# Two Mamba mixers on one core: the second token tile's state part moved ahead of the first tile's sums of squares

## What is computed

```
proj = x @ in_proj            # z (1024), xBC (1024 + 2N), dt (heads)
xBC  = silu(conv4(xBC) + b)   # causal, 4 taps, per channel
dt   = softplus(dt + bias);   state_t = exp(dt*A) * state + dt*x_t B_t
y_t  = C_t . state_t + D*x_t
A:  out = rmsnorm(y * silu(z)) @ out_proj      (16 heads of 64, N = 64)
B:  out = (rmsnorm(y) * silu(z)) @ out_proj    (64 heads of 16, N = 128)
```

## Time and profile before

| | us |
|---|---|
| three executions | 2859.62, 2861.10, 2862.26 (median 2861.1) |
| profiled execution, span | 2859.7 |
| TensorE matmul busy | 2733.3 (96%) |
| TensorE weight load busy | 1845.0 (65%) |
| VectorE busy | 2009.9 (70%) |
| ScalarE busy | 1527.0 (53%) |
| GpSimd busy | 926.1 (32%) |
| mean granted TensorE clock | 0.980 of 2.4 GHz |

### The profile page before, as it was taken

How to read it: one execution, slowest core, us unless ns; L and a number is a source line. 1 busy time by engine, 2 the same in 40 slices (tenths; PEclk the granted TensorE clock), 3 DMA queues, 4 the chain that set the end, 5 groups by cost and what they waited for, 6 DMA issues and landing times. The chain is left out here.

```text
span 2859.7 us, 49906 instructions
## 1 busy us (share of the span) xinstructions
PE 2733.3 (96%) x17464; PEld 1845.0 (65%) x17464; DVE 2009.9 (70%) x3695; ACT 1527.0 (53%) x2418; POOL 926.1 (32%) x614
## 2 busy tenths in 40 slices
PE   7999999999999999996899999999999999997996
PEld 6777766777766665455666666666666666664453
DVE  5666666666666663377788888888888888885267
ACT  3444444445455442341577666766667776665242
POOL 2222223222223321232233444333333334332134
PEclk9999999999999999998999999999999999998998
DMA  4000000000000034145000000000000000022333
GB/s 125 23 23 22 22 22 22 23 28 29 22 22 22 16 121 152 45 147 204 12 23 22 22 22 16 21 22 22 15 15 22 22 22 22 15 95 89 112 118 133
DMA packets 79935, 139.59 MB, mean 49 GB/s; under 512 B 17896, under 2 KB 17896, under 8 KB 78832
## 3 DMA queue, kind: packets, MB, share of 16 engines
q1 hardware_dynamic: 70752, 125.92, 12.9%
q10 hardware_dynamic: 9104, 12.63, 1.4%
HBM read 104.98 MB, written 33.55 MB: 48 GB/s over the span
## 5 line engine op out<-in xcount | busy, mean ns | idle before, releaser
L655 PE MATMUL work<-b_xnT,shared_w 128*128 128x256 f32 x2304 | 545.8, 388 | 1.8 <-DVE b_parts L1192 1.3
L655 PE MATMUL work<-a_xnT,shared_w 128*128 128x256 f32 x2176 | 509.4, 392 | 1.3
L655 PEld LDWEIGHTS work<-b_xnT,shared_w 128*128 128x128 f32 x2304 | 426.1, 191 | 90.6 <-issue 30.1
L655 PEld LDWEIGHTS work<-a_xnT,shared_w 128*128 128x128 f32 x2176 | 419.0, 195 | 73.8 <-issue 12.3
L1232 DVE TENSOR_TENSOR b_decay<-b_decay,b_gt 128x1024 f32<-128x1024 f32 x256 | 351.7, 1395 | 119.3 <-ACT b_decay L943 115.8
L936 ACT ACTIVATE b_decay<-seg 128x1024 f32<-128x1024 f32 x256 | 248.5, 1029 | 112.0 <-PE seg L781 111.8
L943 ACT ACTIVATE b_decay<-b_decay 128x1024 f32<-128x1024 f32 x256 | 266.1, 1073 | 0.0
L1406 POOL TENSOR_TENSOR b_rhs<-b_l_side,of_head 128x1024 fp32r<-128x1024 f32 x32 | 82.0, 2563 | 552.4 <-DVE b_l_side L1201 552.4
L1441 POOL TENSOR_TENSOR a_y<-a_y,a_skip 128x1024 f32<-128x1024 f32 x32 | 90.9, 2840 | 484.1 <-DVE a_y L1221 484.1
L1111 DVE SCALAR_TENSOR_TENSOR shared_cv<-shared_pre,a_conv_w,shared_cv 128x256 f32<-128x256 f32 x432 | 189.7, 482 | 74.6 <-ACT shared_cv L880 68.9
L1111 DVE SCALAR_TENSOR_TENSOR shared_cv<-shared_pre,b_conv_w,shared_cv 128x256 f32<-128x256 f32 x480 | 232.1, 517 | 14.2 <-ACT shared_cv L880 6.3
(11 more groups left out here) (314 smaller groups left out, 4612.4 us busy)
## 6 DMA issues: line engine op xcount, KB each, us to landing
shared_x<-in_L_attn_a_x SPq DMA_DIRECT2D x16, 512.0 KB, 3.5
a_x_res<-in_L_attn_a_x SPq DMA_DIRECT2D x32, 256.0 KB, 2.6
x_mid<-a_x_res SPq DMA_DIRECT2D x32, 256.0 KB, 2.1
shared_w<-in_L_ffn_d_w SPq DMA_DIRECT2D x2, 4096.0 KB, 14.0
f_d_w<-in_L_ffn_d_w SPq DMA_DIRECT2D x2, 4096.0 KB, 14.5
f_x_res<-x_mid SPq DMA_DIRECT2D x8, 1024.0 KB, 5.9
f_bc_w<-x_mid SPq DMA_DIRECT2D x8, 1024.0 KB, 5.6
shared_x<-x_mid SPq DMA_DIRECT2D x16, 512.0 KB, 3.6
```

The costliest lines, as they stand in the source:

```text
L655: mm = nc.tensor.matmul(dst, w_in[:, k, col:col + m], xnT[:, k, :], start=(k == 0), stop=(k == KD - 1))
```

## The change

On TensorE the steps `z0a, z0b, rs0, yoff1a, yoff1b, seg1.0, rt0, out0` become `z0a, yoff1a, yoff1b, rs0, seg1.0, z0b, rt0, out0`. The banks follow from the order. The use two before: for yoff1a it is state0 (state0b in mixer B) instead of z0b, for yoff1b z0a instead of rs0, for rs0 yoff1a instead of z0a, for z0b yoff1b instead of the state step, for rt0 rs0 instead of yoff1a, for out0 z0b instead of yoff1b. ScalarE copies z0b after the two bounds instead of ahead of them. VectorE runs `from_state(1)` ahead of `square_sums`, and in mixer B (NP = 4) the conv of the last two blocks comes after `square_sums` instead of ahead of `from_state`. In the last super-tile, without z and conv work, the order changes from `rs0, yoff1a, yoff1b, seg1.0, rt0` to `yoff1a, yoff1b, rs0, seg1.0, rt0`. No instruction is added or removed.

```diff
@@ -463,8 +463,8 @@
                 if p + 1 == NP:
                     steps += state_steps(0)
                 steps += [f"ydiag0.{2 * p}", f"ydiag0.{2 * p + 1}"]
-            steps += ["z0a", "z0b"] if nxt else []
-            steps += ["rs0", "yoff1a", "yoff1b", "seg1.0", "rt0", "out0"]
+            steps += (["z0a"] if nxt else []) + ["yoff1a", "yoff1b", "rs0", "seg1.0"]
+            steps += (["z0b"] if nxt else []) + ["rt0", "out0"]
             for p in range(NP):
@@ -1005,10 +1005,10 @@
                     square(2 * i)
                     if nxt:
                         z_copy(sec, "z0a")
+                    slot_bound(sec, 1, 0)
+                    slot_bound(sec, 1, 1)
                     if nxt:
                         z_copy(sec, "z0b")
-                    slot_bound(sec, 1, 0)
-                    slot_bound(sec, 1, 1)
                     slot_exp(sec, 1, 0)
                     slot_exp(sec, 1, 1)
                     out_rsqrt(2 * i)
@@ -1313,8 +1313,10 @@
                             if g + 1 == NS and NP > 1:
                                 state_add(sec, 0)
                                 gate(sec, 0)
-                            for k in range(0, len(blks), 2):
-                                conv_blocks(sec, blks[k:k + 2])
+                            late = blks if g + 1 == NS and NP > 1 else []
+                            if not late:
+                                for k in range(0, len(blks), 2):
+                                    conv_blocks(sec, blks[k:k + 2])
@@ -1323,8 +1325,10 @@
                     if NP == 1:
                         state_add(sec, 0)
                         gate(sec, 0)
+                    from_state(sec, 1)
                     square_sums(sec, "rs0")
-                    from_state(sec, 1)
+                    for k in range(0, len(late), 2):
+                        conv_blocks(sec, late[k:k + 2])
                     rms_var(sec, "rt0")
                     slot_mult(sec, 1, 0)
                     slot_mult(sec, 1, 1)
```

## The result

The changed kernel takes 2869.1 us (median of six executions, 2866.7 to 2877.9) against 2861.2 us (six of the kernel before, 2859.5 to 2862.3): a ratio of 1.0031, 95% interval 1.002 to 1.0043. It is slower by 7.9 us. The profiled execution is one of the fastest (2866.7 us, span 2864.9), so its 5.2 us over the span of before are less than the median shows.

A forecast was written before the change was run, and what follows sets the result against it. TensorE, its matmuls busy 96% of the span, was taken as the bound. 19.4 - 1.0 - 6.1 = +12.3 on the profiled 2859.7 gave 2872.0, with 1.4 for the runs' median 2873 us; range 2865 to 2884.

The forecast's parts named there:

- The mechanism in A: Mixer A's 15 super-tiles: yoff1b waits for z0a's copy, out0 for z0b's; loss 1.29 us each, +19.4 us.
- The unseen step: TensorE's step from rs0 to seg1.0, not in the trace: taken as 0.58 us, bounds 0.38 and 1.14.
- Mixer B: Its 15 super-tiles: yoff1b doesn't wait, out0 at 7.17 us after z0a instead of 7.27; -0.07 each, -1.0 us.
- The conv's cover: VectorE in mixer B: the later conv, 3.84 us, even at 1.5 times, ends before out0 has ended; cost 0.
- The last super-tiles: Without z work, state parts fill TensorE's wait for the squares: gain 2.5 us in A, 3.6 in B, 6.1 together.
- The clock in A's loop: Low-clock stretches in 7 of mixer A's 15 super-tiles, 1.69 us each: number left at 7, ±8.4 us.
- rival 2: No change: mixer A's low-clock stretches fall to nearly none, -8 to -12 us, time 2861 to 2866; 12%.
- Rival 3: TensorE's new idle stretch in many of A's super-tiles brings the low clock: up to 25 us more, 2885 to 2898; 12%.
- Rival 1: Mixer A's loss is absorbed by TensorE's headroom, under 0.5 us a super-tile, time 2854; 6%.

The follow-up runs named there:

- B's part alone: The kernel before, with the new order only in mixer B's 15 super-tiles with z work: 2864.0 us, ratio 0.9996.
- dt moved: The changed kernel with mixer A's dt projection behind block 0 of xBC instead of ahead of it: 2861.2 us, ratio 0.9995 to the kernel before.

## Why the prediction was right

The forecast, A pays and the kernel is slower, held: 2869.1 against 2873 predicted, inside 2865 to 2884. By its steps:

- *The mechanism in A.* yoff1b loaded 3.42 us after z0a (forecast 3.45), rs0 4.47 (4.50), seg1.0 5.04 (5.08), z0b 5.48 (5.52), out0 7.94 (8.02), the two releasers as named. 1.21 us a super-tile against 1.29, 18.2 us against 19.4. What I called idle was 0.7 us and the trace's bracket is 1.20, since yoff1a's two loads take 0.29 and its matmuls hide the difference.
- *The unseen step.* rs0 to seg1.0 was 0.57 in both mixers, 0.58 taken from another change of tile shape. Taking the nearest row and not the middle of its bounds made the rest fit.
- *Mixer B.* 0.17 us gained in most super-tiles where I took 0.07; yoff1b did meet z0a's copy, with a bracket of 0.43, as state part and copy ended together. In one super-tile of the profiled execution, B's second, z0a waited 1.68 us for `state_add`, because one rhs instruction on VectorE took 2.9 us beside GpSimd. From B's first out0 to its last but one the profiled execution is 0.9 us shorter, for 1.0 forecast; the kernel with B's part alone differs from the before by -0.04%, less than its interval. The 1.0 is neither confirmed nor refuted.
- *The conv's cover.* I allowed 1.5 times its duration beside GpSimd and it took 2.05 times, and 2.9 times the undisturbed 2.70. I left out that the masks, by then free of GpSimd, would take 1.65 us less. The cover held with 0.9 us to spare.
- *The last super-tiles*: 6.1 forecast with bounds 3 and 9, 6.1 net in the profiled execution (3.0 in A for 2.5, 3.1 in B for 3.6). That this fits so well is luck. The steps that I had worked out gave 2.5 and 3.5; the clock, which I had named only in the bound, gave 2.2 in A's tile 0 and took 1.6 in its tile 1, and B lost 0.4 to the masks. The kernel with this part alone gained 10 us, beyond my bound; 7.4 of it lie in the last super-tiles.
- *The clock in A's loop*: I left the number at 7; it was 4 in the profiled execution, -5.1 us, and so a part of rival 2 came true. Between the two profiled executions, A's 14 distances give +11.96 us, the way to A's first out0 +0.23, the last super-tiles -6.07, B's loop -0.86, and the feed-forward stages -0.06: +5.20, the difference of the spans. The forecast of +12.3 was too high mainly by these three stretches. How many the slower executions had is not known; they were not profiled.
- *Rival 3* did not come. With dt moved, the changed kernel has no low-clock stretch in A's loop, though every super-tile has the new idle time.
- *The range*: I put A's ends at -3 and +6, while my bounds of 15 and 27 around 19.4 are -4.4 and +7.6. With those it would have been about a microsecond wider on each side.
- *Rival 1*, that A's loss is absorbed, was refuted. I had drawn it from a rule of the Trainium skill, Perfetto Trace Analysis, Identifying the Most-Contended Engine, that TensorE's headroom is judged by the busy share of its weight loads (and by its share of peak arithmetic, which I left out). Reading that share as free time fails in this case: weight loads are busy 64 to 65%, and yet out0 coming 1.21 us later cost 1.21 us in every one of the 14 distances. I take it that the slack elsewhere was small and moved along, as I had argued from the 0.5 us of the earlier trace rows; no run tests this by itself.

## What to carry to other kernels

With banks used in turn, moving a step changes who waits for whose copy: write down the use two before for each step of the new order, and where its copy stands in the other engine's queue. A projection that looks like filler may be the cover of a gate, a square and a copy; moving half of it behind exposes them, and where the same move has nothing to uncover (the last super-tile) it gains. Look at the granted clock by short windows too: here moving a group of narrow matmuls behind one wide step gave 8.7 us, more than the 7.9 that the change cost. And give a stage its gain only after following it to the stage's last instruction: in A's last super-tile a low-clock stretch moved and took back part of what was won.

## What the hardware showed that I had not expected

A VectorE instruction with two SBUF inputs can be held for about as long as a GpSimd instruction runs: in mixer B single conv instructions (0.48 us in the median) took up to 2.68 us, one of them 2.58 us and done 0.28 us after a GpSimd instruction of 2.65; six took 7.88, and 2.70 with GpSimd held back. The Trainium skill, GPSIMD Engine Reference, Specifications, says that the two share their SBUF interfaces and that VectorE instructions with two SBUF inputs contend. The runs agree, and add that moving the contention to the masks makes these 4.75 us instead of 2.34.

In A's loop the granted clock stood at 1.2 GHz for 3.4 us at a time right behind the sixteen 16-column matmuls of the dt step, in 7 super-tiles of the kernel before and 4 of the changed one, at a cost of 1.69 us each. With block 0 of xBC ahead of these matmuls it did so in none of four kernels. In mixer B's loop, whose dt matmuls have 64 columns, no such stretch stands in the kernel before. It came in ten super-tiles when 2.9 us of idle time were added elsewhere, and once in the kernel with B's part alone, behind a wait of 1.42 us and the dt step, where the distance grew to 81.5 us from 79.9:

```profile
2494.11 0.52 PEld L723 LDWEIGHTS work<-tri_le,b_aa 128*128 128x128 f32 x4 [1.42 <-DVE b_x_res L1286]
```
```profile
2496.50:2499.50 3.00, 3.00 (x10) 2.13 (x10) 1.69 (x6) 2.21 (x4) 0.00 (x0) 0.50 0.30 87
```
